# A vision-transformer layer in one program: attention scores from q and k split in two parts

## What is computed

```python
q = silu(x @ Wq); k = silu(x @ Wk); v = x @ Wv          # per head
cum = cumsum(-softplus(x @ Wa + ba), axis=1)
decay = exp(where(causal, cum_i - cum_j, -inf))
attn = einsum('bhid,bhjd->bhij', q, k) * decay
o = einsum('bhij,bhjd->bhid', attn, v)
o = (o - mean) / sqrt(var + eps) * gn_w + gn_b           # per head
h = h + (o * sigmoid(x @ Wg)) @ Wo
h = h + moe(layernorm(h))                                # 8 experts, 2 per token
```

## Time and profile before

| | us |
|---|---|
| median of 3 runs (1321.25 to 1325.42) | 1324.96 |
| the profiled execution | 1323.79 |
| its span in the profile | 1321.9 |
| TensorE busy | 1250.9 (95%) |
| TensorE weight loads busy | 1072.3 (81%) |
| ScalarE busy | 858.5 (65%) |
| VectorE busy | 825.2 (62%) |
| GpSimd busy | 428.1 (32%) |

### The profile page before, as it was taken

One profiled execution on the slowest core, in us unless ns is written; L12 is line 12 of the kernel. 1 busy time (PEld: TensorE's weight loads), 2 busy tenths in 40 slices (PEclk: granted clock), 3 DMA queues, 4 the chain that ended last, 5 costly groups with the idle time before them and its releaser, 6 DMA issues. The chain is left out here.

```text
span 1321.9 us, 27298 instructions
## 1 busy us (share of the span) xinstructions
PE 1250.9 (95%) x8534; PEld 1072.3 (81%) x8534; DVE 825.2 (62%) x2119; ACT 858.5 (65%) x2019; POOL 428.1 (32%) x524
## 2 busy tenths in 40 slices
PE   3899999999999999999999999999999999999996
PEld 2676777878778778778778778889999999989996
DVE  4455556665665665665665566657788888565552
ACT  2557577576576576576576565636788888666662
POOL 2021211241241241241141142164444544433434
PEclk7799999999999999999999999999999999999998
DMA  5321331341331331341332236458888787888873
GB/s 193 121 93 61 105 98 47 117 131 46 117 129 49 109 128 57 108 130 57 108 114 63 89 102 186 161 179 245 282 238 222 222 237 188 262 257 262 249 232 88
DMA packets 125607, 194.46 MB, mean 147 GB/s; under 512 B 16272, under 2 KB 91504, under 8 KB 125360
## 3 DMA queue, kind: packets, MB, share of 16 engines
q1 hardware_dynamic: 111920, 175.91, 41.5%
q0 software_dynamic: 13584, 17.26, 6.4%
HBM read 167.40 MB, written 29.05 MB: 149 GB/s over the span
## 5 line engine op out<-in xcount | busy, mean ns | idle before, releaser
L1161 PE MATMUL bank<-xn_sp,big_r 128*128 128x512 f32 x1152 | 312.1, 408 | 0.0
L1161 PEld LDWEIGHTS bank<-xn_sp,big_r 128*128 128x128 f32 x1152 | 204.6, 188 | 53.2 <-issue 1.4
L1674 DVE TENSOR_TENSOR att<-bank,dec_x 128x384 f32<-128x384 f32 x256 | 130.7, 552 | 110.1 <-PE bank L1198 108.9
L817 ACT ACTIVATE dec_x<-dec_x,ncum 128x256 f32<-128x256 f32 (+1 forms) x512 | 189.7, 444 | 5.7 <-POOL dec_x L654 5.7
L654 POOL TENSOR_SCALAR_AFFINE_SELECT dec_x<-dec_x 128x256 f32<-128x256 f32 x256 | 103.6, 434 | 215.8 <-DMA dec_x<-cum_scratch 215.7
L1494 PE MATMUL bank<-big_r 128*128 128x256 f32 x1296 | 168.0, 286 | 1.5 <-ACT mid_f L887 1.0
L1494 PEld LDWEIGHTS bank<-big_r 128*128 128x128 f32 x1296 | 160.5, 192 | 3.3 <-ACT mid_f L887 1.4
L705 POOL TENSOR_SCALAR mid_f<-mid_f,dec_x 128x256 f32<-128x256 f32 x71 | 76.9, 1087 | 187.0 <-DVE mid_f L1925 184.6
L711 POOL DMA_INDIRECT out<-mid_f,tok x71 | 118.6, 1671 | 53.0 <-POOL mid_f L705 22.0
L1941 DVE TENSOR_TENSOR big_r<-mid_f,big_r 128x256 fp32r<-128x256 f32 x216 | 91.4, 424 | 69.5 <-ACT big_r L907 69.3
L887 ACT ACTIVATE mid_f<-bank,h 128x256 f32<-128x256 f32 x216 | 101.2, 477 | 43.5 <-PE bank L1494 22.1
(11 more groups left out here) (217 smaller groups left out, 2231.4 us busy)
## 6 DMA issues: line engine op xcount, KB each, us to landing
big_f<-in_L_ffn_w SPq DMA_DIRECT2D x68, 1024.0 KB, 6.2
dec_x<-cum_scratch SPq DMA_DIRECT2D x128, 384.0 KB, 3.5
big_w<-in_L_ffn_w SPq DMA_DIRECT2D x12, 1024.0 KB, 6.7
mid_f<-expert_rows SPq DMA_DIRECT2D x27, 261.0 KB, 3.4
xt<-in_x SPq DMA_DIRECT2D x16, 256.0 KB, 3.7
h_scratch<-h SPq DMA_DIRECT2D x16, 256.0 KB, 2.3
h<-h_scratch SPq DMA_DIRECT2D x8, 512.0 KB, 4.3
out<-h SPq DMA_DIRECT2D x16, 256.0 KB, 4.0
```

The costliest lines, as they stand in the source:

```text
L817: act.activation(d, d, ACT.Exp, bias=ncum[p % 2][:, NS * u + s, 2 * c + hh:2 * c + hh + 1]).then_inc(M["exp_done"], 1)
L1161: mm = pe.matmul(bank[target][:, :], wp[:, k, c * P:(c + 1) * P], xp[:, k, :], start=(k == 0 and j == 0), stop=(k == EC - 1 and j == 2))
L1674: dve.tensor_tensor(att[hh][:, :], bank[4 + hh][:, 0:LW], dec[n % RING][:, hh, :], ALU.mult).then_inc(M["mult_done"], 1)
```

## The change

It splits q and k in a high part and a low part, and makes the scores of three float32r products. `q_hi` and `k_hi` on ScalarE copy the silu results to the high parts; `q_lo` and `k_lo` on VectorE subtract. Each split operand has two buffers: even head pairs in a tile `qk_sp`, odd ones in `y_sp` 0, whose former user (the low part of the gated output) now lies in `big_lo`, over the gated output itself. `tanh_k` gets a buffer `tk` of its own, in the room of the fourth decay buffer: `RING` is 3. The order of the steps changes on every engine:

- TensorE: Q(c+1), [V], S0, K(c+1), ..., W0, S1, [V], G(c+1), [turn], W1. `turn(2p+2)` moves behind G. Step 7 keeps its order.
- ScalarE: `keep_o`, `decay(c, 1)`, `tanh_q`, ..., `tanh_k`, `q_hi`, `k_hi`, `decay(c+1, 0)`, ..., `tanh_g`.
- VectorE: `head_stats`, `decayed(c, 0)`, `silu_q`, ..., `silu_k`, `q_lo`, `decayed(c, 1)`, `k_lo`, ...; `choose(2p-3)` moves from ahead of `decayed(0, 1)` to behind `embed(2p+2)`.

```diff
-RING = 4
+RING = 3
...
+        qk_sp = sb("qk_sp", [P, 4 * SP2], F32R)
+        q_sp = [[x[:, i * SP2:(i + 1) * SP2] for i in range(2)] for x in (qk_sp, ys[0])]
+        k_sp = [[x[:, i * SP2:(i + 1) * SP2] for i in range(2, 4)] for x in (qk_sp, ys[0])]
         tq = sb("tq", [P, SP2])
-        dec_x = sb("dec_x", [P, RING * 2 * LW])
+        dec_x = sb("dec_x", [P, RING * 2 * LW + SP2])
+        tk = dec_x[:, RING * 2 * LW:RING * 2 * LW + SP2]
...
             def ahead(p, c, u):
-                if c + 2 < NP:
-                    load_decay(p, c + 2, u)
+                d = c + 1 + u
+                if d < NP:
+                    load_decay(p, d, 1 - u)
...
                 for c in range(NP):
                     q, d = (p, c + 1) if c + 1 < NP else (p + 1, 0)
+                    if main:
+                        decay_rows(p, c, 1)
                     if pair(q):
                         decay_rows(q, d, 0)
-                        decay_rows(q, d, 1)
...
+            def q_hi(p, c):
+                n = NP * p + c
+                act.wait_ge(M["sq_done"], n + 1)
+                have(act, "s_ps", 4 * (n - 1))
+                act.activation(q_sp[c % 2][0], tq[:, :], ACT.Copy).then_inc(M["qh_done"], 1)
...
             def scores(p, c, u):
                 n = 4 * (NP * p + c) + 2 * u
-                pe.wait_ge(M["sq_done"], NP * p + c + 1)
-                pe.wait_ge(M["sk_done"], NP * p + c + 1)
+                pe.wait_ge(M["ql_done"], NP * p + c + 1)
+                pe.wait_ge(M["kl_done"], NP * p + c + 1)
                 have(pe, "mult_done", n)
-                q, k = (x[c % 2][:, u * S:(u + 1) * S] for x in (q_s, k_s))
-                for hh in range(2):
-                    r = slice(D * hh, D * hh + D)
-                    pe.matmul(bank[4 + hh][:, 0:S], k[r, 0:P], q[r, :], start=True, stop=True)
...
+                qs, ks = ([x[:, u * S:(u + 1) * S] for x in y[c % 2]] for y in (q_sp, k_sp))
+                for j, (k, q) in enumerate(three(ks, qs)):
+                    for hh in range(2):
+                        r = slice(D * hh, D * hh + D)
+                        pe.matmul(bank[4 + hh][:, 0:S], k[r, 0:P], q[r, :], start=(j == 0), stop=(j == 2))
+                for j, (k, q) in enumerate(three(ks, qs)):
+                    for hh in range(2):
+                        r = slice(D * hh, D * hh + D)
+                        mm = pe.matmul(bank[4 + hh][:, S:LW], k[r, P:S], q[r, P:S], start=(j == 0), stop=(j == 2))
...
+            def q_lo(p, c):
+                n = NP * p + c
+                dve.wait_ge(M["qh_done"], n + 1)
+                dve.tensor_tensor(q_sp[c % 2][1], tq[:, :], f32(q_sp[c % 2][0]), ALU.subtract).then_inc(M["ql_done"], 1)
```

More of the change, by code:

```diff
@@ L136, in vit_layer @@
         wt = sb("wt", [P, KT + 1, E])
+        with nc.sbuf_tensor("big_lo", [P, 8192], F32R) as big_lo:
+            pass
         big_f = sb("big_f", [P, 8192])
@@ L210, in vit_layer @@
         w1_stage = [w1_f[0], w1_x]
-        gel_u = [x[:, i * BLK:(i + 1) * BLK] for x in q_s + k_s for i in range(2)]
+        gel_u = [gel_w[:, i * BLK:(i + 1) * BLK] for i in range(HC)]
         gel_1 = [gel_u[c // 2][:, (c % 2) * P:(c % 2 + 1) * P] for c in range(HC)]
@@ L473, in _ @@
                             store_h(2 * p + 3)
-                        if c == 6:
-                            store_cum(p + 1)
                     ahead(p, c, 0)
+                    if c == 6 and pair(p + 1):
+                        store_cum(p + 1)
                     if c == 0 and pair(p + 1):
@@ L910, in last_step @@
                 main, nxt = pair(p), pair(p + 1)
+                if main:
+                    keep_o(p, 6)
                 if nxt:
@@ L913, in last_step @@
                 if main:
+                    decay(p, 7, 1)
                     y_hi(p, 0, 0)
-                    keep_o(p, 6)
                     if p == NPR - 1:
@@ L921, in last_step @@
                     keep_v(p + 1, 0, 2)
-                    decay(p + 1, 0, 0)
+                    q_hi(p + 1, 0)
                 if main:
@@ L939, in step @@
                     keep_o(p, c - 1)
+                if c == 2 and nxt:
+                    keep_xnT(2 * p + 2)
                 if c == 4 and nxt:
@@ L944, in step @@
                 if main:
+                    decay(p, c, 1)
                     tanh_q(p, c + 1)
[L946 to L947 removed]
+                    for i, source in {0: ((2, 1), (3, 2)), 1: ((4, 2),), 3: ((7, 2),)}.get(c, ()):
                         keep_v(p, i, source)
@@ L958, in step @@
                     tanh_k(p, c + 1)
+                    q_hi(p, c + 1)
+                if c == 6 and nxt:
+                    keep_cum(p + 1)
+                if main:
+                    k_hi(p, c + 1)
+                    if c in (1, 2):
+                        keep_v(p, c + 4, 0)
                 if c == 6 and post:
@@ L1388, in step @@
                     scores(p, c, 1)
-                    keys(p, c + 1)
                 if c == 0 and post:
                     gn_var(p - 1, 1)
-                if c == 1 and nxt:
-                    turn(2 * p + 2)
                 if c == 1 and main:
@@ L1407, in step @@
                     gates(p, c + 1)
+                if c == 1 and nxt:
+                    turn(2 * p + 2)
                 if c == 3 and nxt:
@@ L1663, in silu_k, with k_lo @@
                 dve.wait_ge(M["tk_done"], n + 1)
-                have(dve, "s_ps", 4 * (n - 1))
-                dve.scalar_tensor_tensor(out=k_s[c % 2][:, :], in0=tq[:, :], scalar=1.0, in1=bank[1][:, :],
+                dve.scalar_tensor_tensor(out=tk[:, :], in0=tk[:, :], scalar=1.0, in1=bank[1][:, :],
                                          op0=ALU.add, op1=ALU.mult).then_inc(M["sk_done"], 1)
+            def k_lo(p, c):
+                n = NP * p + c
+                dve.wait_ge(M["kh_done"], n + 1)
+                dve.tensor_tensor(k_sp[c % 2][1], tk[:, :], f32(k_sp[c % 2][0]), ALU.subtract).then_inc(M["kl_done"], 1)
             def decayed(p, c, u):
@@ L1961, in last_step @@
                 if nxt:
+                    q_lo(p + 1, 0)
                     silu_k(p + 1, 0)
+                    k_lo(p + 1, 0)
                 if post and main and p < NPR - 1:
@@ L1986, in step @@
                         head_stats(p, c - 1)
+                    decayed(p, c, 0)
                     silu_q(p, c + 1)
-                if c == 0:
-                    if post:
-                        spread(p - 1, 1)
-                    if routed:
-                        choose(2 * p - 3)
+                if c == 0 and post:
+                    spread(p - 1, 1)
                 if c == 1 and nxt:
@@ L2010, in step @@
                 if main:
+                    silu_k(p, c + 1)
+                    q_lo(p, c + 1)
                     decayed(p, c, 1)
@@ L2014, in step @@
                 if main:
-                    silu_k(p, c + 1)
+                    k_lo(p, c + 1)
                 if c == 0:
@@ L2020, in step @@
                         embed(2 * p + 2)
+                    if routed:
+                        choose(2 * p - 3)
                     if p == NPR - 1:
```

74 lines of the change are left out of this document (35 added, 39 removed).

## The result

| | before | after |
|---|---|---|
| median, us | 1325.19 (4 runs, 1321.25 to 1327.13) | 1375.26 (4 runs, 1370.86 to 1377.55) |
| span of the profiled execution | 1321.9 | 1375.1 |
| TensorE busy | 1250.9 | 1284.2 |
| mean granted clock of TensorE | 0.983 | 0.963 |

The change makes the kernel slower: ratio 1.0378, 95% interval 1.034 to 1.0415, some 50 us. The forecast was 1366.7 with a range of 1320 to 1398. TensorE's busy time grows by 33.3 us and its idle time by the other 19.9 us of the span.

A forecast was written before the change was run, and what follows sets the result against it. The prediction took TensorE's stream to bound the kernel (busy 100.29 of 102 us per pair). Terms -1.7 + 10.0 + 15 + 11.2 + 7 + 1.4 = +42.9 on 1323.8 gave 1366.7 us, range 1320 to 1398.

The forecast's parts named there:

- S with three products, 0.84: TensorE's scores block: narrow passes cost their weight load, 0.11 us, so 0.84 in place of 0.85; -1.7 us over 128 blocks.
- The rate-of-columns rival: Scores block: narrow and wide passes run at the rate of their columns, -17 us, total 1349; chance 0.04.
- The rival of loads that nothing hides: Scores block: weight loads not hidden in the split array, S 1.29 us, +58 to the sum, about 1410; chance 0.08.
- The order, +0.21 in six steps: TensorE, steps 1 to 6 of 8 pairs: one more array change in each direction, 0.21 us per step, +10.0 us.
- Steps 0 and 1, +15: V4 after step 0, pairs 2 to 6: waits for tanh_g behind top_exp, which waits for choose; 3.0 x 5 = +15 us.
- Step 3, +11.2: turn, pairs 0 to 6: waits for embed_norm late on VectorE; 1.7 x 6, and 1.0 for pair 0, +11.2 us.
- Step 5, +7: W1, pairs 0 to 6: waits for decayed(5, 1), late on VectorE behind softplus and tanh_k; 1.0 x 7 = +7 us.
- No wait of TensorE for `silu_q` or `silu_k` is among its waits.: TensorE's waits before the change: hence having two heads' K or Q ready earlier buys nothing.
- Step 7, +1.4: W1, pairs 0 to 6: waits for decayed(7, 1), about 0.6 us in place of 0.4; +1.4 us.
- The added work, counted at nothing on average: Two copies on ScalarE (0.64 us), two subtractions on VectorE (0.70) per step; room on average, nothing in the sum there.
- The first rival: ScalarE's and VectorE's queues keep up and old waits go: 1320 us, with cheap narrow passes 1303; chance 0.16.
- The second: Rival: only part of the waits come, half of the 34.6 us; about 1349, between 1329 and 1352; chance 0.17.

The follow-up runs named there:

- experiment 7: On top of experiment 3, the second half of the scores' matmuls got all 256 columns of q in place of 128; 1337.71 us, ratio 1.0066 to 1.0113.
- experiment 5: On top of experiment 3, S0 put back directly behind W1, ahead of Q; 1339.25 us, ratio 1.0082 to 1.0132.
- experiment 8: Changed kernel with embed_rsqrt(2p+3) on GpSimd moved behind the mask of decay(3, 1); 1356.18 us, ratio 1.0214 to 1.0271.
- Experiment 10: Kernel before with turn(2p+3) moved to step 4, keep_xnT behind the decay of step 5, and keep_o(p, 6) first on ScalarE in step 7; 1312.36 us.
- Experiment 4: Changed kernel with unread matmuls added, 7 ahead of the waiting V and 8 ahead of the waiting turn; 1357.72 us, ratio 1.0223 to 1.0289.
- Experiments 3: Changed kernel with top_exp of step 0 behind tanh_g, turn(2p+3) in step 4 behind K and keep_xnT behind q_hi; 1336.2 us, ratio 1.0065 to 1.013.
- experiment 6: On top of experiment 3, only two of the three products in the scores; 1325.68 us (10 runs), ratio 0.998 to 1.0012.

## Why the prediction was right, and where it was not

The sign, the size and the two main places were right. The sum of 42.9 stands against 53.2 in the span, but that it comes this near is partly luck, since two errors have opposite signs: the waits were counted too high by some 14 us (4.7 in step 1, 1.5 in step 5, 5.0 in step 7 and 4.2 for an old wait that the change ends, less some 1 too few in step 3, from the points below), and the clock was not counted at all, 20 to 24 us.

- **S with three products, 0.84.** Right: the median over the traced blocks is 0.836. That a pass of 128 columns costs its weight load was taken from a row with 16 columns; experiment 7 shows for this kernel that its columns don't set its time. The rate-of-columns rival falls, and with it the 81 ns of the Trainium skill, "TensorE: Matmul & The Clock Gate", section "Back-to-back issue gap". That page's load time in the section "LDWEIGHTS (loading the stationary operand)", columns divided by 1.2 GHz, gives 107 ns for 128 columns, and the trace agrees, with 0.106 in the earlier trace rows and an S that needs 0.11. The rival of loads that nothing hides, S of 1.29, falls too.
- **The order, +0.21 in six steps.** Right where the stream can be seen alone: step 2 grew by 0.14 to 0.18, with 0.03 taken off by the two S, and experiment 5 gave 0.22 back there. Over the steps it was less than +10.0: step 4 grew by 0.12, and step 6 by about 0.1, counted without the two waits of the kernel before that are gone from it (0.61 ahead of S0, 0.1 ahead of W0).
- **Steps 0 and 1, +15.** The mechanism was right, `choose` behind `embed` and `tanh_g` behind `top_exp`; the size was off. My walk had `top_exp`'s input at 14.1 us from the step's start and V4 3.0 late. It came at 13.6, and step 1 has 2.05 more than without the wait: 10 us in five pairs. The other 1.5 of step 1 is clock.
- **Step 3, +11.2.** The place and chain were right: `turn` starts at 11.7 where I had 11.2. The 1.0 per pair for the mask behind `embed_rsqrt`, which I had kept for the range alone, belonged in the sum: experiment 8 measures 1.28. That `turn` came so near to my 11.2 is luck: with the mask out of the way it starts at 10.3, so my walk of VectorE's queue was 0.9 too long, and the mask I had left out made up for it. `turn`'s waits over pairs 0 to 6 are 12.2 us more than before, where I had 11.2. The step costs 2.31 where the clock holds, 3.3 to 3.5 where it doesn't, and step 4 another 1.7 to 2.1.
- **Step 5, +7.** Right in place, and near in size. The step grew by 0.95, of which the order is 0.2 and the wait of W1 for `decayed(5, 1)` nearly 0.8 (0.43 ahead of it and 0.37 between its heads), 5.5 us in seven pairs. W1 could start at 8.0 where I had 8.1; the products were done at 8.7 where I had 9.2.
- **"No wait of TensorE for `silu_q` or `silu_k` is among its waits."** Wrong. Of the 1.7 us of idle time in a pair I gave a cause to 1.2. The other 0.5 was S0 of step 6 waiting for `silu_k`, which the profile calls `issue`; with Q ahead of S0 it is gone. So K ready earlier did buy something: 4.2 us in seven pairs that the sum doesn't have.
- **Step 7, +1.4.** Wrong in its sign: -0.5 in a step. I priced the wait of W1 for `decayed`, and overlooked that `keep_o(p, 6)` now comes first on ScalarE, which takes W0's 0.4 us wait of the earlier trace rows away. Experiment 10 gives this to the kernel before: -0.45.
- **The clock.** No step of the prediction had it. The clock rows of the kernel before showed 1.00 throughout a pair, and the waits that I forecast had no like in them. Experiment 4 is what shows it.
- **The added work, counted at nothing on average.** It came due where the prediction looked for it, at the ends of two queues. Experiments 3, 5 and 6 add that once those two waits are gone, VectorE bounds steps 1, 3 and 5.

The first rival, queues that keep up, fails on its own conditions: V waits 2.1 to 2.3 us for `tanh_g(1)`, `turn` 2.5 to 2.9 for `embed_norm`. The second, half of the 34.6 us of waits, came nearer than the forecast where it spoke of waits: net they are some 20 us. Without the fall of the clock the kernel would have come out at some 1351 to 1355, where that rival (1349) and the low end of the forecast (1352) meet.

What stays open: why the clock holds through step 3 in pair 4 of the changed kernel (10.73 busy of 13.60) and falls in pair 3 (11.23 of 14.10). I found no difference in the work of the two. The expert blocks' 1.7 us, for which the sum had nothing, were not tested. The trace of the kernel after has a wait of 3.6 us for expert rows there, and behind it 6.8 us at half speed from 1195.6 us on; the kernel before has neither.

## What to carry to other kernels

Before work is added to an engine that is idle a third of the time, walk its queue up to the places where the busiest engine waits for it: what lies last in the queue there decides, and here two placements gave back 39 of 50 us. Give every idle stretch of the busiest engine a cause before you count on it, also one that the profile puts down to `issue`: the change may end that wait, as it did 4.2 us here. Price a wait of the busiest engine above its length where it is repeated every few steps, since the clock may fall with it. And splitting a product with few columns into three cheaper ones may gain nothing: S took 0.84 us in place of 0.85.

## What the runs showed of the hardware

- **Repeated waits of TensorE of 2 to 3 us were followed by stretches at 1.2 GHz.** With waits of 2.3 for V and 2.9 for `turn`, 54.6 us at half speed; without the first, 37.5; with the first kept and the second cut to 1.6 to 1.8, 20.5; with both waits filled by unread matmuls, 10.2; the kernel before 6.8. The loss was as large as the waits: 20 to 24 us beside 19.9 of added idle time. Adding 7 and 8 matmuls of no use made the kernel 17.5 us faster.
- **The work behind a wait pays, not the wait.** Step 4 waits for nothing and takes 17.1 to 17.6 us in place of 15.5 in the five pairs whose clock fell in or behind step 3.
- **Row-split float32r passes.** Two heads on the two halves of the rows load and run side by side: a block S of twelve matmuls with twelve loads takes 0.84 us, where twelve loads of 0.106 one behind the other would take 1.27. Each product left out saved 0.23 (one wide and one narrow pass of both heads), and doubling the narrow pass's columns cost 0.02 a pass.
